# Graph layers before a routed FFN: two unread 512-column matmuls behind every group's products in layer one

## The chip, the cores and the metric

The kernel runs on one core of a Trainium2 chip. The metric is the device time of one launch in microseconds. The kernel before takes 6100.4 us, the median of three runs (6088.14, 6100.40 and 6104.39 us). The engines are called by their profile names: PE (TensorE), DVE (VectorE), ACT (ScalarE), POOL (GpSimd) and SP (SyncE).

## The reference

The input is x with 12500 nodes of 256 features, and 200000 edges sorted by destination, each with a source, a destination and a weight. What is computed, in float32:

```
def _gcn_layer(x, W, b, edge_weight, edge_src, edge_dst):
    support = x @ W
    msgs = support[edge_src] * edge_weight[:, None]
    agg = jax.ops.segment_sum(msgs, edge_dst, num_segments=N_NODES)
    return agg + b
h = elu(_gcn_layer(layernorm(x), W1, b1, ...)); h = elu(_gcn_layer(h, W2, b2, ...)); x = x + h
H = gelu(layernorm(x) @ ffn_W1 + b1)             # 1024 wide
probs = softmax(H @ Wg + bg); expert = argmax(probs)   # 8 experts
x = x + probs[expert] * (H @ Wd[expert] + bd[expert])
```

## The kernel before

The kernel applies the weights after the sum over edges, so a layer first sums the weighted source rows of each destination and then multiplies by W.

**Groups.** The edges are cut into 392 groups of 512 (`GE`), processed from the highest destination to the lowest. The `rows` tile has 8 slots (`SLOTS`), one for each group in flight. For every group POOL issues four indirect DMAs (L537), each of which gathers 128 rows of 256 floats from `xn_scratch` (layer one) or `h_scratch` (layer two) into the group's slot. Before the four it waits on L534 until the group that used the slot before, eight groups earlier, has been multiplied (semaphore `s_mm`).

**Products.** DVE builds four matrices S of 128 edges by 96 destinations (L853, `build_S`). PE multiplies them with the gathered rows, eight matmuls of 96 columns a group (L1170, `products`), into one of two banks of `pA`; the last one raises `s_mm`. DVE then adds the bank into the window of 192 numbers a partition in `aggT` (L892) and builds S for the group two further on. PE's products for a group wait for its rows, its S, and for the add of two groups earlier (L1226 to L1234). If a group's destinations go beyond its window, an extra product and add follow (`overflow`, the branch with `with_overflow`); the trace shows no time in that part that the argument needs.

**Halves and ticks.** Four groups make a half, of which a layer has 98 (`NH`). After a half every engine may run ticks, one for a block of 128 nodes whose sums are complete: layer one has one tick a half nearly everywhere. In a tick of layer one ACT copies the block into `stage` (L630) after the last add of the half, PE multiplies it with W1 into `pZ` (L1180, two matmuls of 256 columns), and ACT and DVE do bias and elu of the block before and store it through SP to `h_scratch`. PE's tick stands behind the half's fourth products and ahead of the next half's first ones. In layer two a tick also carries the FFN's first matmul, the gate and the stores. After both layers the nodes are sorted by expert and the second FFN matmul runs (L1282, L1292).

Each engine's program is written out in its own order, and semaphores join them. The two PSUM banks of `pB` hold the transposed edge tables before layer one (L1154) and the FFN's hidden block in layer two (L1208); layer one itself uses neither.

Of the kernel before, what the change touches and what calls it, by code (L numbers as in the profile page):

```python
# [7 lines left out]
def bass_gnn_then_routed_ffn(  # L8
# [92 lines left out]
    with ctx:  # L101
        def sb(name, shape, dt=f32):
            return ctx.enter_context(nc.sbuf_tensor(name, shape, dt))

        def ps(name, shape):
            return ctx.enter_context(nc.psum_tensor(name, shape, f32))
# [21 lines left out]
        w1 = sb("w1", [P, KC, HID])  # L128
# [5 lines left out]
        ident = sb("ident", [P, P])  # L134
# [80 lines left out]
        pB = ps("pB", [P, 1024])  # L215
# [141 lines left out]
        def half_flags(eng, h):  # L357

            v = eng.value_load(regs[0:1, bass.ds(h, 1), 0], min_val=0, max_val=(1 << 17) - 1)  # L359
            return v >> 16, (v >> 8) & 255, v & 255  # L360

        def overflow_windows(eng, g):
            ws = eng.value_load(wins[0:1, bass.ds(g, 1), 0], min_val=0, max_val=NG * P)
            we = eng.value_load(wins[0:1, bass.ds(g, 1), 1], min_val=0, max_val=NG * P)
            return ws, we
# [217 lines left out]
        def _(act):  # L583
# [89 lines left out]
            for layer in range(2):  # L673
                with act.Fori(0, ITERS) as i:
                    for half in range(2):
                        h = 2 * i + half
                        _, start, end = half_flags(act, h)
                        ticks(act, start, end, lambda j: (tick1, tick2)[layer](j, h))
                if layer == 0:
                    tick1(NB, None)  # L680
# [449 lines left out]
        def _(pe):  # L1130
            mm = nc.tensor.matmul
# [5 lines left out]
            for c in range(GCH):  # L1137
                cnt = P if c < GCH - 1 else TAILG
                at = NG - c * P - cnt
                for to, vector in zip(pROW, (gvec(0), gvec(1), gvec(3))):  # L1140
                    last = mm(to[:, at:at + cnt], vector[0:cnt, c:c + 1], flip[0:cnt, P - cnt:P],
                              start=True, stop=True)
# [4 lines left out]
            n = 0  # L1147
# [18 lines left out]
            def products(slot, Sx, to, semaphore):  # L1166

                for k in range(KC):
                    for t in range(T):
                        last = mm(to[:, k * W:(k + 1) * W], rows[:, slot, t, k * P:(k + 1) * P], Sx[:, t, :],  # L1170
                                  start=(t == 0), stop=(t == T - 1))
                last.then_inc(semaphore, 1)

            def z_part(layer, j):

                wg = (wg1, wg2)[layer]
                pe.wait_ge(s_stage[layer], j + 2)
                pe.wait_ge(s_zb[layer], j + 2)
                for k in range(KC):
                    last = mm(pZ[:, 0:C], stage[:, k, :], wg[:, k, :], start=(k == 0), stop=(k == KC - 1))  # L1180
                last.then_inc(s_z[layer], 1)

            def tick1(j):
                z_part(0, j)

            def tick2(j):
# [24 lines left out]
                if flows(0, j):  # L1211
                    z_part(1, j)
# [10 lines left out]
            def edges_half(layer, i, h, half, with_overflow):  # L1223
                for u in range(HALF):
                    s, g = half * HALF + u, HALF * h + u
                    pe.wait_ge(s_gath[layer][s], 16 * T * (i + 1))  # L1226
                    if with_overflow:
                        ws, we = overflow_windows(pe, g)
                        with pe.If(ws < we):
                            with pe.Fori(ws, we) as w:  # L1230
                                pe.wait_ge(s_ovS[layer], w + 1)
                                products(s, Sov, pOV, s_ovmm[layer])
                    pe.wait_ge(s_S[layer], g + 1)
                    pe.wait_ge(s_add[layer], g + 1)  # L1234
                    products(s, S[:, s % 2, :, :], pA[:, s % 2, :], s_mm[layer])

            pe.wait_ge(s_w, 8 * 16)
            for layer in range(2):
                with pe.Fori(0, ITERS) as i:
                    for half in range(2):  # L1240
                        h = 2 * i + half
                        ovf, start, end = half_flags(pe, h)
                        with pe.If(ovf > 0):
                            edges_half(layer, i, h, half, True)
                        with pe.Else():
                            edges_half(layer, i, h, half, False)
                        ticks(pe, start, end, (tick1, tick2)[layer])
# [16 lines left out]
            for i in runs(pe, NB // (2 * LB)):  # L1264
                for n in range(2):
                    pe.wait_ge(s_tile, 2 * i + n + 1)
                    pe.wait_ge(s_tgate, 2 * i + n + 1)
                    for k in range(LB):
                        outer = isinstance(i, int)
                        last = mm(pL, lane_is[:, n, k, :], tile_is[:, n, k, :, :].rearrange("p v n -> p (v n)"),  # L1270
                                  start=(outer and i == 0 and n == 0 and k == 0),
                                  stop=(outer and i > 0 and n == 1 and k == LB - 1))
# [53 lines left out]
```

## Time and profile before

| | us |
|---|---|
| median of three runs | 6100.4 |
| the profiled execution's own time | 6100.27 |
| its span, first to last instruction | 6098.5 |
| layer one, from POOL's first gather | about 95 to 2535 |
| layer two | about 2535 to 5500 |
| sorting and experts | about 5500 to 6098 |

Busy shares of the span are PE 59%, PE's weight loads 55%, POOL 53%, DVE 33% and ACT 18%. The profile's time starts at the first instruction. A busy time of PE counts from an instruction's start to a modelled end, and each float32 matmul of the program shows as two records, so a group's eight matmuls are 16 records. An "x64" on L1170 is the products of four groups. The number in brackets behind a row of the timeline is the engine's idle time just ahead of it, with what ended it; "remote" means that the releaser's record was not found.

### The profile page before, as it was taken

The numbers are of one execution on the slowest core, as the hardware profiler recorded it, in microseconds if no ns is written. First come the engines' busy times: TensorE is split into PE (matmuls) and PEld (weight loads), VectorE is DVE, ScalarE is ACT, GpSimd is POOL, SyncE is SP. The second block draws the span as 40 slices with busy tenths as digits, with TensorE's granted clock in tenths as the row PEclk, the third lists the DMA queues.
The fourth block names the chain that finished last, engine by engine and source line by source line (L and its number), as shares of the span: only waits on it lengthen the run. The fifth ranks groups of instructions, "written<-read, shape, count | busy, mean of one in ns | idle before, by whom it ended". The sixth has DMA issues, their size and how long they took to land.

```text
span 6098.5 us, 84880 instructions
## 1 busy us (share of the span) xinstructions
PE 3582.9 (59%) x21458; PEld 3351.2 (55%) x21459; DVE 2006.6 (33%) x6596; ACT 1122.0 (18%) x1692; POOL 3256.1 (53%) x3403
## 2 busy tenths in 40 slices
PE   2455555455555545466556556555656555566999
PEld 2454445444544445465555555555556555565888
DVE  6222222222222222233333333333333333336333
ACT  3111111111111111032222222222222222221111
POOL 5566666566666666545555445545555554542444
PEclk6666666666666666677777777777777777778999
DMA  7333333333333333223333333333333333323554
GB/s 235 87 94 91 91 92 92 88 93 91 92 93 89 92 89 93 77 81 97 99 96 98 96 100 95 97 94 98 97 97 96 97 97 95 97 84 108 179 177 157
DMA packets 266659, 627.26 MB, mean 103 GB/s; under 512 B 63397, under 2 KB 135034, under 8 KB 265922
## 3 DMA queue, kind: packets, MB, share of 16 engines
q0 software_dynamic: 170688, 492.87, 27.9%
q1 hardware_dynamic: 95362, 129.30, 6.0%
q14 instruction: 597, 4.89, 0.3%
q8 instruction: 12, 0.20, 0.0%
HBM read 519.25 MB, written 103.63 MB: 102 GB/s over the span
## 4 chain that ended last, share of the span: by engine, by line
issue 30%; PE 25%; another core or an unknown queue 21%; DVE 10%; DVEq 9%; ACT 3%; ACTq 1%; DMA 1%; POOL 0%; SPq 0%; POOLq 0%
PE pA L1170 12%; PE pA L1292 6%; DVE S L853 4%; PE pB L1208 3%; DVEq L359 1%; DVEq L882 1%; PE pZ L1180 1%; DVE aggT L892 1%; DVEq L853 1%; DVEq L892 1%; DVEq L975 1%; PE pC L1282 1%; PE pB L1282 1%; DVEq L370 1%
## 5 line engine op out<-in xcount | busy, mean ns | idle before, releaser
L537 POOL DMA_INDIRECT rows<-h_scratch,idx x1568 | 1488.8, 949 | 1474.3 <-PE pA L1170 830.9
L1170 PE MATMUL pA<-S,rows 128*128 128x96 f32 x12544 | 1891.1, 323 | 509.0 <-DVE S L853 331.2
L1170 PEld LDWEIGHTS pA<-S,rows 128*128 128x128 f32 x12544 | 1850.2, 238 | 593.7 <-DVE S L853 442.7
L537 POOL DMA_INDIRECT rows<-xn_scratch,idx x1568 | 1491.9, 951 | 924.2 <-issue 429.0
L892 DVE TENSOR_TENSOR aggT<-aggT,pA 128x192 f32 x784 | 277.4, 354 | 3280.6 <-remote 1591.5
L630 ACT ACT_TABLE_LOAD x196 | 251.5, 1283 | 4195.9 <-DVE aggT L892 2838.8
L853 DVE TENSOR_SCALAR S<-iota_p,tdst,twgt 128x96 f32<-128x96 f32 x3152 | 861.1, 343 | 12.3 <-issue 9.1
L1180 PE MATMUL pZ<-wg,stage 128*128 128x256 f32 x784 | 311.1, 537 | 855.5 <-ACT stage L630 609.4
L1180 PEld LDWEIGHTS pZ<-wg,stage 128*128 128x128 f32 x784 | 186.5, 263 | 896.1 <-ACT stage L630 621.2
L1208 PE MATMUL pB<-work,w 128*128 128x128 f32 x3232 | 592.6, 361 | 72.5 <-issue 71.2
L1198 PE MATMUL pT<-ident,work 128*128 128x128 f32 x206 | 67.9, 431 | 943.8 <-DVE work L930 703.4
L1208 PEld LDWEIGHTS pB<-work,w 128*128 128x128 f32 x3232 | 568.5, 274 | 82.8 <-issue 81.5
L1198 PEld LDWEIGHTS pT<-ident,work 128*128 128x128 f32 x206 | 29.1, 196 | 963.9 <-DVE work L930 717.8
L1292 PE MATMUL pA<-aggT,work 128*128 x1680 | 382.9, 381 | 0.2
L1292 PEld LDWEIGHTS pA<-aggT,work 128*128 128x128 f32 x1680 | 312.1, 191 | 40.5 <-issue 1.1
L567 POOL DMA_INDIRECT out_dram<-aggT,ids x105 | 107.3, 1022 | 227.3 <-DVE ids L1093 180.5
L1192 PE MATMUL pC<-identg,work 128*128 128x136 f32 x1236 | 166.3, 283 | 22.7 <-issue 20.2
L1192 PEld LDWEIGHTS pC<-identg,work 128*128 128x128 f32 x1236 | 152.7, 191 | 24.0 <-issue 21.2
L1111 DVE TENSOR_TENSOR aggT<-pA,aggT 128x256 f32<-128x256 f32 x105 | 44.6, 425 | 277.2 <-PE pA L1292 222.9
L669 ACT ACT_TABLE_LOAD x100 | 128.3, 1283 | 8.2 <-remote 6.4
L658 ACT ACT_TABLE_LOAD x100 | 128.3, 1283 | 1.8
L935 DVE TENSOR_TENSOR work<-pB,b1col 128x1024 f32<-128x1024 f32 x102 | 123.9, 1214 | 3.3 <-PE pB L1208 2.4
(173 smaller groups left out, 2286.3 us busy)
## 6 DMA issues: line engine op xcount, KB each, us to landing
pay_scratch<-work SPq DMA_DIRECT2D x98, 512.0 KB
rows<-xn_scratch,idx POOLq DMA_INDIRECT x1568
rows<-h_scratch,idx POOLq DMA_INDIRECT x1568
h_scratch<-work SPq DMA_DIRECT2D x98, 128.0 KB
pay_scratch<-work SPq DMA_DIRECT2D x98, 128.0 KB
work<-in_x_dram SPq DMA_DIRECT2D x97, 128.0 KB
rows<-in_x_dram SPq DMA_DIRECT2D x24, 512.0 KB, 5.3
xn_scratch<-rows SPq DMA_DIRECT2D x24, 512.0 KB, 5.7
```

The source lines that it names most:

```text
L537: pool.indirect_dma_start(rows[:, s, t, :], None, source, bass.IndirectOffsetOnAxis(at, 0))\
L630: act.activation(stage[:, :, :], aggT[:, :, block_of(j)], ACT.Copy).then_inc(s_stage[layer], 1)
L658: act.activation(bstd[:, 0:1], bmv[:, 1:2], ACT.Sqrt, bias=epsc[:, :]).then_inc(s_std2, 1)
L669: act.activation(HT, hid, ACT.Gelu).then_inc(s_gelu, 1)
L853: last = v.tensor_scalar(S[:, half, t, :], iota_w[:, :], tdst[:, t, bass.ds(g, 1)], twgt[:, t, bass.ds(g, 1)], ALU.is_equal, ALU.mult)
L892: v.tensor_tensor(to, to, pA[:, u % 2, 0:KC * W].rearrange("p (k n) -> p k n", k=KC), ALU.add)\
L935: v.tensor_tensor(hid, pB[:, :].rearrange("p (k n) -> p k n", k=KH), b1col[:, :].unsqueeze(2).to_broadcast([P, KH, P]), ALU.add).then_inc( ...
L1170: last = mm(to[:, k * W:(k + 1) * W], rows[:, slot, t, k * P:(k + 1) * P], Sx[:, t, :], start=(t == 0), stop=(t == T - 1))
L1180: last = mm(pZ[:, 0:C], stage[:, k, :], wg[:, k, :], start=(k == 0), stop=(k == KC - 1))
L1192: mm(pF[:, m // PERB, m % PERB, :], HT[:, m, :], identg[:, m, :], start=True, stop=True)
L1208: last = mm(pB[:, m * P:(m + 1) * P], w1[:, k, m * P:(m + 1) * P], xnT[:, k, :], start=(k == 0), stop=(k == KC - 1))
L1292: last = mm(pA[:, q % 2, 0:C], HTx[:, q % 2, m, :], wdk[:, m, bass.ds(ec, C)], start=(m == 0), stop=(m == KH - 1))
```

## The change

A function `keep_running` is added, and in layer one PE calls it behind the products of each group. It multiplies the 128x128 identity matrix with the first 1024 columns of `w1`, in two matmuls of 512 columns, into the two banks of `pB`. Nobody waits for them and nobody reads what they write; they raise no semaphore and wait for none. The group's `s_mm` is still raised by the last matmul of the products ahead of them. The call stands in `edges_half`, in both branches.

```
+            def keep_running():
+
+                for n in range(2):
+                    mm(pB[:, n * 512:(n + 1) * 512], ident[:, :], w1[:, 0, n * 512:(n + 1) * 512], start=True, stop=True)
+
@@
                     pe.wait_ge(s_S[layer], g + 1)
                     pe.wait_ge(s_add[layer], g + 1)
                     products(s, S[:, s % 2, :, :], pA[:, s % 2, :], s_mm[layer])
+                    if layer == 0:
+                        keep_running()
```

The first place is on PE, inside a half of layer one without overflow: the end of the skipped branch, then the first two groups. Before:

```order
L1243 UNCONDITIONAL_BRANCH
L1226 ISA
L1233 REGISTER_ALU
L1170 MATMUL pA<-S,rows 128x96 x8
L1233 REGISTER_ALU
```

And after, with the lines below the new function moved down:

```order
L1250 UNCONDITIONAL_BRANCH
L1231 ISA
L1238 REGISTER_ALU
L1170 MATMUL pA<-S,rows 128x96 x8
L1177 MATMUL pB<-w,ident 128x512 x2
L1238 REGISTER_ALU
```

The second group's wait for its rows (the `REGISTER_ALU` with the gather's semaphore) and its products now stand behind two matmuls of 512 columns.

The second place is on PE at the end of a half, where `pZ<-wg,stage` is the tick's matmul. Before:

```order
L1233 REGISTER_ALU
L1170 MATMUL pA<-S,rows 128x96 x8
L1245 UNCONDITIONAL_BRANCH
L369 REGISTER_ALU x3
L369 COMPARE_AND_BRANCH
L370 UNCONDITIONAL_BRANCH
L370 ISA
L1180 MATMUL pZ<-wg,stage 128x256 x2
```

And after:

```order
L1238 REGISTER_ALU
L1170 MATMUL pA<-S,rows 128x96 x8
L1177 MATMUL pB<-w,ident 128x512 x2
L1252 UNCONDITIONAL_BRANCH
L369 REGISTER_ALU x3
L369 COMPARE_AND_BRANCH
L370 UNCONDITIONAL_BRANCH
L370 ISA
L1185 MATMUL pZ<-wg,stage 128x256 x2
```

The fourth group's extra matmuls stand between its products and the tick, whose matmul waits for `stage` in both kernels. The order on DVE, ACT, POOL and SP is unchanged.

## Rows read from the trace of the kernel before

**Rows 1.** The page's head: busy time of PE, and granted clock by slice.

```profile
span 6098.5 us, 84880 instructions
...
PEclk6666666666666666677777777777777777778999
```

**Rows 2.** Busy by stage; last three columns: granted clock, DMA share, GB/s.

```profile
95.00:2535.00 2440.00, 1259.40 (x6664) 1159.74 (x6664) 675.59 (x2411) 269.42 (x493) 1488.63 (x1566) 0.67 0.32 91
2535.00:5500.00 2965.00, 1764.19 (x11731) 1696.46 (x11732) 993.84 (x3324) 718.20 (x976) 1488.49 (x1568) 0.76 0.31 95
```

**Rows 3.** Groups of layer one: busy, mean ns, idle before, releasers.

```profile
L537 POOL DMA_INDIRECT rows<-xn_scratch,idx x1565 | 1488.8, 951 | 915.8 <-issue 420.6 <-PE pA L1170 290.8 <-remote 194.3
L1170 PE MATMUL pA<-S,rows 128*128 128x96 f32 x6272 | 1066.3, 350 | 336.1 <-DVE S L853 230.3 <-DVE aggT L892 77.2 <-issue 27.1
L1180 PE MATMUL pZ<-wg,stage 128*128 128x256 f32 x392 | 203.0, 673 | 855.5 <-ACT stage L630 609.4 <-issue 170.7 <-DVE zb L901 75.3
L892 DVE TENSOR_TENSOR aggT<-aggT,pA 128x192 f32 x392 | 138.3, 353 | 1617.5 <-remote 782.7 <-PE pA L1170 460.8 <-issue 374.0
```

**Rows 4.** Timeline of one half of layer one: start, length, what, idle before.

```profile
1536.91 0.35 DVE L892 TENSOR_TENSOR aggT<-aggT,pA 128x192 f32 x1 [5.80 <-remote]
...
1537.50 0.95 POOL L537 DMA_INDIRECT rows<-xn_scratch,idx  x1 [2.44 <-remote]
...
1539.29 2.08 PE L1180 MATMUL pZ<-wg,stage 128*128 128x256 f32 x4 [10.25 <-ACT stage L630]
...
1541.16 9.26 PE L1170 MATMUL pA<-S,rows 128*128 128x96 f32 x64
1541.26 0.95 POOL L537 DMA_INDIRECT rows<-xn_scratch,idx  x1 [0.30 <-issue]
1544.95 0.35 DVE L892 TENSOR_TENSOR aggT<-aggT,pA 128x192 f32 x1 [4.09 <-PE pA L1170]
...
1545.52 0.95 POOL L537 DMA_INDIRECT rows<-xn_scratch,idx  x1 [3.30 <-PE pA L1170]
...
1547.02 0.35 DVE L892 TENSOR_TENSOR aggT<-aggT,pA 128x192 f32 x1 [0.53 <-PE pA L1170]
...
1550.52 0.95 POOL L537 DMA_INDIRECT rows<-xn_scratch,idx  x1 [0.30 <-issue]
1551.40 0.35 DVE L892 TENSOR_TENSOR aggT<-aggT,pA 128x192 f32 x1 [3.07 <-PE pA L1170]
...
1559.30 0.95 POOL L537 DMA_INDIRECT rows<-xn_scratch,idx  x1 [0.30 <-issue]
1562.71 0.35 DVE L892 TENSOR_TENSOR aggT<-aggT,pA 128x192 f32 x1 [9.95 <-remote]
```

**Rows 5.** Stretches of that half; columns as in Rows 2.

```profile
1541.20:1544.70 3.50, 3.50 (x18) 3.50 (x18) 0.00 (x0) 0.00 (x0) 0.95 (x1) 0.50 0.39 115
1544.70:1550.40 5.70, 5.70 (x49) 5.55 (x47) 2.86 (x10) 0.00 (x0) 3.79 (x4) 0.95 0.25 70
1545.00:1547.00 2.00, 2.00 (x19) 2.00 (x18) 1.49 (x5) 0.00 (x0) 1.18 (x2) 0.94 0.00 0
1547.00:1561.90 14.90, 3.41 (x31) 3.25 (x29) 2.67 (x10) 0.00 (x0) 10.20 (x11) 0.67 0.37 106
1562.00:1564.00 2.00, 0.00 (x0) 0.00 (x0) 1.29 (x6) 0.67 (x1) 0.70 (x1) 0.50 0.00 0
```

**Rows 6.** L1180 in layer one: duration ns, least, median, most.

```profile
L1180 PE MATMUL pZ<-wg,stage x392: 597/634/796, 150.8 to 2526.5; 128*128 128x256 f32 x196
```

**Rows 7.** L1292 in the experts' stage, 256 columns; columns as in Rows 3.

```profile
L1292 PE MATMUL pA<-aggT,work 128*128 x1680 | 382.9, 381 | 0.2
```

**Rows 8.** Timeline of layer two; columns as in Rows 4.

```profile
4025.08 3.81 PE L1170 MATMUL pA<-S,rows 128*128 128x96 f32 x32 [1.29 <-DVE S L853]
...
4031.61 0.35 DVE L892 TENSOR_TENSOR aggT<-aggT,pA 128x192 f32 x1 [5.33 <-remote]
...
4032.20 0.95 POOL L537 DMA_INDIRECT rows<-h_scratch,idx  x1 [0.94 <-remote]
```

## The prediction

> **What bounds the kernel now.** I read the busy time by stage first. Layer one takes 2440 us from POOL's first gather, with PE busy for 1259 us, a mean granted clock of 0.67 and the DMA engines at 32% [rows 2]. Neither PE nor the DMA engines fill it; clock and span are those of [rows 1].
>
> Then the groups of that stage. POOL's 1565 gathers there have 1488.8 us busy and 915.8 us idle [rows 3]. A gather is 0.951 us, and the usual gap behind it is 0.30 us [rows 4], so the 16 gathers of a half cost 20.0 us if nothing stops them. A half really takes (1488.8 + 915.8) / 1565 x 16 = 24.6 us. So POOL's issue is the base of the time, and about 4.6 us a half, 450 us in 98 halves, are stops of POOL. It stops only for a free slot, and slots are freed by PE's `s_mm`.
>
> Then one half in order of time [rows 4]. Call its groups g0 to g3. The last add of the half before starts at 1536.91, and POOL resumes at 1537.50. ACT stages the block, PE starts the tick's matmul at 1539.29 and the products of g0 at 1541.16; DVE adds g0 at 1544.95 and POOL resumes at 1545.52, after a stop of 3.30 us. PE goes straight through all four groups, 64 records in 9.26 us, so it is done at 1550.4. POOL meanwhile issues twelve gathers without a stop, to 1560.25. The add of g3 comes at 1562.71, 12.3 us after PE's last record, and with it the next half starts. So a half is: add of g3, to g0's products seen (8.0 us between POOL's two restarts), three groups of gathers, and the wait until g3 is seen.
>
> The reader is to see that finished products are noticed at once in some places and late in others. With 16 records each, at 3.50 us for 18 of them and then 5.70 us for 49 [rows 5], g0 ends at about 1544.6, g1 at 1546.7, g2 at 1548.6 and g3 at 1550.4. A waiting add starts some 0.2 us after it is released. So g0 and g1 are seen at once (adds 1544.95, 1547.02), g2 about 2.6 us late (1551.40) and g3 12 us late. The DMA engines moved nothing from 1545.0 to 1547.0, 106 GB/s from 1547.0 to 1561.9, and nothing after 1562 [rows 5]: g1 is noticed in a pause of the gathers, g2 and g3 ended while gathers were landing. Layer two has the same: 32 records start at 4025.08 and last 3.81 us, so the first group of the two ends near 4027.1, its add comes only at 4031.61, and POOL, which had stopped for it, resumes at 4032.20 [rows 8]. That is 4.3 us late. "Remote" as releaser of 782.7 us of DVE's waits for adds [rows 3] fits this.
>
> The Trainium skill says in "Perfetto Trace Analysis", section "Tensor Engine Instruction (MATMUL, LD_WEIGHTS)", that TensorE's ends are estimated and that the semaphore update leaves when PSUM has acknowledged the writes. The trace agrees that the two differ, by up to 12 us in the half above; the page gives no cause and no figure for it.
>
> **The change part by part.** Nothing is removed. Each group gets two float32 matmuls of 512 columns, four records. At the high clock the nearest row is the experts' 256-column matmul, 382.9 us / 1680 = 0.228 us a record [rows 7]; twice the columns is 0.456, so 1.8 us a group. At the low clock it is the tick's matmul, also 256 columns, 203.0 / 392 = 0.518 us [rows 3], so 4.1 us a group. In the half above the clock is 0.50 during g0 and 0.95 from 1544.7 on [rows 5]. So I take 2.1 us behind g0 (0.5 us of it low) and 1.8 us behind g1 to g3, 7.5 us a half. PE is busy 1259 / 98 = 12.9 us of 24.6 now [rows 2], so the work itself fits: 20.4 of 24.6.
>
> *Behind g3.* The extra 1.8 us lie in the time in which PE waits for the stage, 10.25 us ahead of the tick [rows 4]. Cost nothing; if g3 were seen at once, 2.4 us (add to tick's matmul) would still cover them.
>
> *Behind g2.* They delay g3. g3 ends near 1550.4 now and is needed by POOL at 1560.3. Covered by 10 us.
>
> *Behind g0.* They delay the products of g1, whose wait for rows and whose matmuls are queued behind them on PE. g0's own `s_mm` is raised before them. g1 ends at 1548.8 instead of 1546.7. POOL needs g1 for its gather at 1550.52, so by about 1550.2. If it is seen at once, the cost is 0, the lower bound. But the pause of the gathers is over at 1547.0, and g1 now ends where g2 did. With g2's lateness of 2.6 us it is seen at 1551.4 to 1551.5, and POOL resumes 0.8 us later (4031.4 to 4032.20 in layer two): 1552.3 instead of 1550.52, +1.8 us. With layer two's 4.3 us it is +3.5 us, the upper bound. I take g2's lateness as the nearest row, and in 60% of the halves, since the slack of 1.4 us covers the smaller delays: 1.1 us a half.
>
> *Behind g1.* g2 starts up to 1.8 us later than its place behind g1. POOL needs it a group of gathers later than g1, 5.0 us, and is itself later by then. Nothing in the forecast; in the rival with every group late it costs.
>
> *The clock.* Extra work on PE could hold the high clock over the wait, so that the tick's matmul and g0 run faster: 2.08 / 2 = 1.0 us, and for g0 3.3 - 1.9 = 1.4 us, together 2.4 us a half off the stop of 3.30. The rows speak against it: over 1547.0 to 1561.9 the clock is 0.67 [rows 5], which is 5 us high and 10 low, so it fell near 1552, within 2 us of PE's end. The 392 records of L1180 in layer one have a least duration of 597 ns [rows 6], against 381 ns mean for as many columns at the high clock [rows 7]. PE's idle time before the tick shrinks from 12 us ahead of this add by 7.5 us at most, and stays longer than what the clock survived here. I take 0.
>
> In "TensorE: Matmul & The Clock Gate", section "Why this matters for your kernels", the Trainium skill says to keep TensorE continuously busy for the high clock and without long gaps between bursts. That speaks for the change: with the gap filled, the sum would be 98 x 2.4 us less, the first rival. The trace agrees with it on the fall after idleness, and no row here shows whether the shorter gap is short enough.
>
> **The sum.** Made against the profiled execution, 6100.3 us (span 6098.5 and 1.8 around it), which is the median of the runs within 0.1 us. 98 x 1.1 = 108 us, all in layer one; layer two has no added work. 6100 + 108 = 6208 us. With the bounds of g1's cost, 0 and 3.5 us, it is 6100 to 6443.
>
> **Rivals.**
> - *The clock stays high through the tick (faster).* For it: less idle time ahead of the tick. Against it: [rows 5, 6] as above. It decides from the point where the clock is high at the tick's matmul; 2.4 x 98 = 235 us less, 5865 us.
> - *g3 is seen early (faster).* If what follows on PE brings a finished group to notice, the extra matmuls behind g3 do that, and the tick hides beside POOL's gathers: 24.6 falls to 20.0 + 0.6, 98 x 4.0 = 392 less, 5708 us. Against it: g2 has work right behind it now and is late, in both layers.
> - *All hidden.* g1 is seen within its slack of 1.4 us: 6100 us.
> - *Every group is late.* With g1 seen in the flow, g2 and g3 each bring a stop of their own as in layer two, 0.94 - 0.30 = 0.6 us each: 1.8 + 0.6 + 0.6 = 3.0 us a half, 294 us, 6394 us.
> - *PE becomes the bound.* If the clock stayed low, a half on PE is 4 x (3.3 + 4.1) + 2.1 + 2.4 = 34.1 us, 9.5 more: 931 us, 7030 us. Against it: the clock rises now with less work on PE.
>
> **How the numbers follow.** Forecast 0.43 (own range 6130 to 6290), high clock 0.09, g3 early 0.04, all hidden 0.17, every group late 0.23, PE the bound 0.04. A measurement of this kernel tells about 0.3%, 18 us, from no change. So faster 0.13, same 0.18 (all hidden and the forecast's edge), slower 0.69. The range runs from 6085, which takes in the hidden case, to 6400, which takes in the case of every group late; left out are the two faster rivals, the bound PE and edges, less than 2 in 10.
>
> **What would show it.** Right: L1177 with 1568 records in layer one, near 0.45 to 0.6 us apart; the add of g1 later by 3 us or more after g0's, and a stop of POOL before its gathers behind g1 that isn't there now; L1180 still with durations near 634 ns; layer two unchanged. Wrong: POOL's idle time in layer one at 916 us or below, L1180 with a median near 400 ns (the clock), or the add of g3 soon after its products.

## The result and the profile after

The changed kernel takes 6119.6 us (median of 12 runs, 6113.0 to 6139.4), the kernel before on the same chip 6103.1 us (12 runs, 6087.7 to 6115.1). The ratio is 1.0034, 95% interval 1.0022 to 1.0045: 17 us slower, where 108 were forecast. Both profiled executions lie off those medians, the one before 3 us under it (6100.3) and the one after 12 us over it (6131.8), so the traces differ by 32 us and the medians by 17.

The page's head after the change, which answers to [rows 1]:

```profile
span 6130.1 us, 88016 instructions
...
PE 4080.0 (67%) x23026; PEld 3438.5 (56%) x23027; DVE 2010.8 (33%) x6596; ACT 1121.3 (18%) x1692; POOL 3247.1 (53%) x3403
...
PEclk7878888888788888777777777777777777778999
```

The two layers, columns as in [rows 2] (after the length: busy us of PE, weight loads, DVE, ACT and POOL, then granted clock, DMA share, GB/s):

```profile
95.00:2560.00 2465.00, 1765.88 (x8212) 1254.58 (x8213) 673.41 (x2386) 264.60 (x485) 1482.55 (x1564) 0.82 0.31 89
2560.00:5535.00 2975.00, 1761.29 (x11764) 1693.53 (x11764) 999.80 (x3351) 723.47 (x986) 1485.42 (x1568) 0.77 0.31 95
```

And the groups of layer one, which answer to [rows 3], with the duration of the tick's matmul, which answers to [rows 6]:

```profile
L537 POOL DMA_INDIRECT rows<-xn_scratch,idx x1564 | 1482.6, 948 | 958.2 <-issue 424.7 <-PE pA L1170 305.9 <-remote 218.5
L1170 PE MATMUL pA<-S,rows 128*128 128x96 f32 x6260 | 904.5, 306 | 108.7 <-issue 50.0 <-DVE S L853 47.2 <-DVE aggT L892 10.6
L1177 PE MATMUL pB<-w,ident 128*128 128x512 f32 x1564 | 805.7, 640 | 0.7 <-issue 0.7
L1185 PE MATMUL pZ<-wg,stage 128*128 128x256 f32 x388 | 175.4, 598 | 609.5 <-ACT stage L630 515.2 <-issue 69.1 <-DVE zb L901 25.2
```

```profile
L1185 PE MATMUL pZ<-wg,stage x388: 379/634/796, 152.1 to 2530.5; 128*128 128x256 f32 x194
```

Three things are to be seen. PE has 507 us more of busy time in layer one and its mean clock there rises from 0.67 to 0.82. The tick's matmul now has a least duration of 379 ns where it had 597, but its median stays at 634 ns: only some ticks find a high clock. And POOL's idle time in layer one goes from 915.8 to 958.2 us, 42 us more, while its busy time there is 6 us less; together that is 36 us, and the traces differ by 32. So the loss is again where [rows 3] had the whole slack: in POOL's stops for a free slot.

**Where the stops lie.** From the start times of L537's 1568 records I took every half, from its first group's first gather to the next half's, and every gap that exceeds the usual 0.30 us by more than 0.3. A half can have such a stop ahead of each of its four slots, and it waits there for g0, g1, g2 or g3 of the half whose slots it takes over. Mean stop by slot, in us, over 96 halves:

| | first (g0) | second (g1) | third (g2) | fourth (g3) | sum |
|---|---|---|---|---|---|
| before | 3.10 | 0.06 | 0.30 | 0.98 | 4.4 |
| after | 2.80 | 0.10 | 0.77 | 1.15 | 4.8 |

The forecast's stop, at the second slot, is not there: 2 halves had one before, 4 have one now. What grew is the stop at the third slot. It is in 46 halves instead of 21. The stop at the fourth slot grew as well in this pair of traces, by 0.17 us, and the one for g0 shrank by 0.30.

Here is a half of the kernel after with it (start, length, what, idle time before it and its releaser, as in [rows 4]; some rows left out):

```profile
1137.30 0.94 POOL L537 DMA_INDIRECT rows<-xn_scratch,idx  x1 [2.90 <-PE pA L1170]
1138.10 1.92 PE L1170 MATMUL pA<-S,rows 128*128 128x96 f32 x16
...
1139.85 1.91 PE L1177 MATMUL pB<-w,ident 128*128 128x512 f32 x4
1140.35 0.35 DVE L892 TENSOR_TENSOR aggT<-aggT,pA 128x192 f32 x1 [7.29 <-PE pA L1170]
...
1141.58 0.34 DVE L892 TENSOR_TENSOR aggT<-aggT,pA 128x192 f32 x1
1141.71 2.02 PE L1170 MATMUL pA<-S,rows 128*128 128x96 f32 x16
...
1145.32 1.92 PE L1170 MATMUL pA<-S,rows 128*128 128x96 f32 x16
1146.06 0.95 POOL L537 DMA_INDIRECT rows<-xn_scratch,idx  x1 [0.30 <-issue]
...
1148.86 0.35 DVE L892 TENSOR_TENSOR aggT<-aggT,pA 128x192 f32 x1 [5.84 <-remote]
...
1149.43 0.95 POOL L537 DMA_INDIRECT rows<-xn_scratch,idx  x1 [2.42 <-remote]
1150.09 0.34 DVE L892 TENSOR_TENSOR aggT<-aggT,pA 128x192 f32 x1
...
1161.55 0.94 POOL L537 DMA_INDIRECT rows<-xn_scratch,idx  x1 [2.41 <-PE pA L1170]
```

g1 and its add are in time (1141.58). g0's add comes 3 us after POOL went on by the same semaphore; there it is DVE that is late, whose sequencer stands 3.6 and 1.8 us behind the branches between two halves (L975, L979), so g0's notice is dated by POOL and not by its add. g2's products start at 1141.71, when the unread matmuls behind g1 and g2's own S (complete at 1141.67) are both done, so only a part of its delay is the change's. g2 ends on PE at 1143.7, 6.4 us after POOL resumed, and is added only at 1148.86. POOL had come to the third slot at 1147.0 and stood still for 2.42 us. In that stop g3 is noticed too (its add is at 1150.09, 2.8 us after its products), so the fourth slot costs nothing, and the next stop is 2.41 us. The half takes 24.25 us.

What the DMA engines moved around that stop, columns as in [rows 5]:

```profile
1143.70:1147.30 3.60, 3.60 (x22) 2.64 (x21) 0.00 (x0) 0.00 (x0) 2.69 (x3) 1.00 0.38 109
1147.30:1148.20 0.90, 0.90 (x3) 0.38 (x3) 0.00 (x0) 0.00 (x0) 0.00 (x0) 1.00 0.45 127
1148.20:1149.40 1.20, 0.79 (x2) 0.00 (x0) 0.54 (x3) 0.00 (x0) 0.00 (x0) 1.00 0.04 14
```

The last gathers land for a microsecond more, then the transfers cease, and within it the two late groups are noticed. "Noticed" is not to be taken as one engine looking too late: the waits of POOL and of DVE for g2's semaphore end at the same moment, 1148.68, as they do for g3 in [rows 4], 1562.55. The signal itself comes late.

And a half of the same kernel with the other kind of stop:

```profile
1536.24 0.95 POOL L537 DMA_INDIRECT rows<-xn_scratch,idx  x1 [3.23 <-PE pA L1170]
...
1542.18 1.92 PE L1170 MATMUL pA<-S,rows 128*128 128x96 f32 x16
...
1550.04 0.95 POOL L537 DMA_INDIRECT rows<-xn_scratch,idx  x1 [0.30 <-issue]
1553.33 0.35 DVE L892 TENSOR_TENSOR aggT<-aggT,pA 128x192 f32 x1 [11.06 <-remote]
...
1553.92 0.94 POOL L537 DMA_INDIRECT rows<-xn_scratch,idx  x1 [2.93 <-remote]
...
1561.37 0.35 DVE L892 TENSOR_TENSOR aggT<-aggT,pA 128x192 f32 x1 [4.10 <-PE pA L1170]
...
1561.94 0.94 POOL L537 DMA_INDIRECT rows<-xn_scratch,idx  x1 [3.33 <-PE pA L1170]
```

Here g3's products start at 1542.18 and end near 1544, no stop comes in the flow, and g3 is noticed 9 us late, when POOL stops for it ahead of the fourth slot (2.93 us). Only then can the tick begin, and the stop for g0 is 3.33 us. The half takes 25.70 us.

**Kinds of half.** Sorted by that, over 95 halves (count x mean us of one):

| | second slot | third only | third and fourth | fourth only | neither | mean |
|---|---|---|---|---|---|---|
| before | 2 x 25.2 | 11 x 24.2 | 10 x 25.5 | 32 x 25.5 | 40 x 23.9 | 24.66 |
| after | 4 x 25.3 | 32 x 24.3 | 13 x 26.0 | 30 x 25.9 | 16 x 24.1 | 25.04 |

A half with a stop at the third slot alone is only 0.2 to 0.3 us longer than one without, since the stop for g0 behind it is shorter, and 1.3 to 1.6 us shorter than one that stops at the fourth slot. The half in [rows 4], on which the forecast was built, starts with POOL's restart at 1545.52 and stops at the fourth slot alone:

```profile
1563.30 0.95 POOL L537 DMA_INDIRECT rows<-xn_scratch,idx  x1 [3.05 <-remote]
...
1570.90 0.95 POOL L537 DMA_INDIRECT rows<-xn_scratch,idx  x1 [2.90 <-PE pA L1170]
```

It takes 25.38 us and is of a dear kind, which a third of the halves belong to in both kernels. What has become rare is the cheapest kind, without a stop in the flow, of which the forecast had no example.

### The profile page after: what moved, and what is told of

It reads as the page before. It is cut to its first block, busy times and chain, and to the rows that moved or that the text cites. A ratio compares the mean times of both kernels' runs of the same rounds, so it can differ in the third digit from the quotient of the medians.

```text
span 6130.1 us, 88016 instructions
## 1 busy us (share of the span) xinstructions
PE 4080.0 (67%) x23026; PEld 3438.5 (56%) x23027; DVE 2010.8 (33%) x6596; ACT 1121.3 (18%) x1692; POOL 3247.1 (53%) x3403
## 4 chain that ended last, share of the span: by engine, by line
PE 38%; another core or an unknown queue 22%; issue 21%; DVE 10%; DVEq 5%; ACT 3%; DMA 1%; ACTq 1%; POOL 0%; SPq 0%; POOLq 0%
PE pA L1170 17%; PE pB L1177 7%; PE pA L1299 6%; DVE S L853 4%; PE pB L1213 3%; PE pZ L1185 3%; DVE aggT L892 1%; DVEq L882 1%; DVEq L853 1%; DVEq L892 1%; PE pC L1289 1%; ACT stage L630 1%; PE pB L1289 1%; DVEq L359 1%
## 5 line engine op out<-in xcount | busy, mean ns | idle before, releaser
L537 POOL DMA_INDIRECT rows<-h_scratch,idx x1568 | 1485.4, 947 | 1474.7 <-PE pA L1170 809.4
L1170 PEld LDWEIGHTS pA<-S,rows 128*128 128x128 f32 x12544 | 1710.5, 218 | 533.8 <-issue 309.0
L537 POOL DMA_INDIRECT rows<-xn_scratch,idx x1568 | 1486.6, 948 | 967.3 <-issue 433.7
L1170 PE MATMUL pA<-S,rows 128*128 128x96 f32 x12544 | 1740.7, 302 | 306.8 <-DVE S L853 180.7
L1177 PE MATMUL pB<-w,ident 128*128 128x512 f32 x1568 | 807.6, 640 | 0.7 <-issue 0.7
L1185 PE MATMUL pZ<-wg,stage 128*128 128x256 f32 x784 | 282.7, 496 | 610.3 <-ACT stage L630 516.0
L1213 PE MATMUL pB<-work,w 128*128 128x128 f32 x3232 | 579.4, 356 | 64.8 <-issue 62.1
L1185 PEld LDWEIGHTS pZ<-wg,stage 128*128 128x128 f32 x784 | 170.9, 242 | 711.1 <-ACT stage L630 582.1
L1177 PEld LDWEIGHTS pB<-w,ident 128*128 128x128 f32 x1568 | 295.6, 210 | 211.6 <-issue 211.6
```

Of the source, the lines that this page charges most:

```text
L537: pool.indirect_dma_start(rows[:, s, t, :], None, source, bass.IndirectOffsetOnAxis(at, 0))\
L1177: mm(pB[:, n * 512:(n + 1) * 512], ident[:, :], w1[:, 0, n * 512:(n + 1) * 512], start=True, stop=True)
L1213: last = mm(pB[:, m * P:(m + 1) * P], w1[:, k, m * P:(m + 1) * P], xnT[:, k, :], start=(k == 0), stop=(k == KC - 1))
```

## The experiments

Kernels that are compared ran in one session on one chip, together with the kernel before, and ratios are to it. There were two sorts of session, and what could be told apart depended on them: in two the kernel before takes 4711 and 4726 us, in the others 6103 to 6203 us. In the fast sort finished products are noticed at once, and POOL has next to no stops in layer one to gain or lose.

**One part of the change at a time, in a session of the fast sort (kernel before 4726.3 us).** The call gets a condition on the group, `u == 3`, `u < 3`, `u == 0`, `u == 1`:

```
-                    if layer == 0:
+                    if layer == 0 and u == 3:
                         keep_running()
```

Behind the fourth group alone:

> The two extra matmuls stand behind the fourth group of a half (g3) alone, 98 places in place of 392. Theory A (the change is a sum of two small terms: g2's products later, which adds 0.48 us of POOL stops a half, and a faster tick in some halves, which takes 0.26 us): the first term is gone, so -5 to -25 us against before, if the 1.8 us behind g3 alone are enough to lift the clock at the tick; else 0. Theory B (the forecast's: g1 is noticed late at 1.8 us a half, and a gain of the clock of nearly the same size hides it): the gain stands alone, -80 us or more. Theory C (none of the places matters, the 17 us are a property of the whole): within 10 us of the full change.

Behind the first three:

> The extra matmuls stand behind g0, g1 and g2 and not behind g3. Theory A: g2's delay is all there, and the idle time of PE ahead of the tick is 1.8 us longer than with the full change: +20 to +55 us against before, more than the full change, with the tick's matmul at the low clock nearly everywhere. Theory B: +100 us. Theory C: as the full change, +17 us.

Behind the first alone:

> The extra matmuls stand behind g0 alone. g1 is delayed by about 2 us, g2 hardly, since it waits for its S. Theory A: -10 to +15 us against before. Theory B (g1 seen late, +1.8 us in most halves): +60 to +110 us, with POOL's stops ahead of the gathers into g1's slot.

Behind the second alone:

> The extra matmuls stand behind g1 alone, so g1's end stays and g2 may start up to 1.8 us later, but only as far as it does not wait for its S anyway. Theory A: 0 to +25 us against before, all of it in stops ahead of the gathers into g2's slot. Theory B: 0.

Measured, in that order: 4724.8 us, ratio 0.9995 (0.9984 to 1.0006); 4731.9, 1.0009 (0.9995 to 1.0024); 4726.0, 1.0002 (0.9990 to 1.0015); 4731.8, 1.0007 (0.9996 to 1.0017). POOL's gathers in layer one with the first of them:

```profile
L537 POOL DMA_INDIRECT rows<-xn_scratch,idx x1565 | 1486.2, 950 | 476.7 <-issue 471.5 <-PE pA L1170 5.2
```

Of 476.7 us idle 471.5 are the usual gaps. A half is 20.06 us, the 20.0 us of POOL's issuing that the forecast worked out. What follows: where products are noticed at once the extra matmuls cost nothing that can be told from noise (all four intervals take in 1). Of the forecast only its lower bound, no cost if g1 is seen at once, could be judged here, and it holds.

**Size of the edit, and the tick (kernel before 6198.6 us).** In a session of the slow sort: the kernel before once more, the whole change, four unread matmuls behind each group in place of two, and ten behind the fourth group alone.

```
-                for n in range(2):
-                    mm(pB[:, n * 512:(n + 1) * 512], ...)
+                for n in range(4):
+                    b = n % 2
+                    mm(pB[:, b * 512:(b + 1) * 512], ...)
```

> The kernel before, for its trace under the conditions of the four runs so far, in which it took 4726 us and not 6103. Theory P (where finished products are noticed at once, POOL's issue sets the pace of layer one): the adds start 0.2 us after the products' end, POOL has next to no stops, and a half is 16 x 1.255 = 20.1 us, layer one about 1968 us. Rival: products are noticed as late as in the first trace, and the gathers are what is faster. If this run takes about 6100 us instead, late notice is back and its trace is one more of that kind.

> The full change, in one call with the kernel before. Theory P: where before takes 4726 us, PE's extra 7.5 us a half lie in PE's waits for gathers, so 0 to +10 us; where before takes 6100 us, +17 us again. Rival Q (each extra matmul costs its own small price, whatever the pace of the rest): +17 us, 0.3%, in both.

> Four extra matmuls behind every group in place of two. A half then needs of PE 4 x (1.8 + 3.6) + 1.0 for the tick + 2.4 from the last add to the tick's matmul = 25 us, above the 20.1 us of POOL's issue. Theory P: where before takes 4726 us, PE becomes the bound: +4 to +6 us a half, 390 to 590 us. Where before takes 6100 us: a half is 24.6 us already and loses 1 to 5 us, 100 to 500 us. Rival (the extra matmuls run beside the products): under 30 us in either.

> Ten extra matmuls behind g3 alone, 9 us at the high clock, to fill PE's wait ahead of the tick. Where before takes 6100 us: the tick's matmul and g0 run at the high clock nearly everywhere and the forecast's first rival is tested: -2.4 us a half, -235 us, if faster products are noticed sooner; 0 if their notice hangs on POOL's gathers. Where before takes 4726 us: g3 is noticed at once, so 9 us of unread work stand ahead of the tick; a half on PE is 4 x 1.8 + 9 + 1 = 17 us plus its waits, +0 to +2.5 us a half, up to 250 us.

Measured: the kernel before 6197.9; the whole change 6208.5, ratio 1.0024 (1.0010 to 1.0039), so the result repeats; with four 6258.8, 1.0100 (1.0070 to 1.0129); with ten behind the fourth 6249.3, 1.0075 (1.0047 to 1.0102). Stops by slot and kinds of half:

| | first | second | third | fourth | second slot | third only | third and fourth | fourth only | neither |
|---|---|---|---|---|---|---|---|---|---|
| before | 3.08 | 0.04 | 0.44 | 1.31 | 1 | 24 | 2 | 45 | 23 |
| whole change | 2.76 | 0.07 | 0.99 | 1.10 | 3 | 44 | 0 | 39 | 9 |
| four | 2.65 | 0.50 | 0.96 | 1.32 | 35 | 32 | 3 | 24 | 1 |
| ten, fourth only | 3.06 | 0.01 | 0.24 | 2.07 | 0 | 9 | 10 | 63 | 13 |

The gathers' rows of layer one for these four, in this order:

```profile
L537 POOL DMA_INDIRECT rows<-xn_scratch,idx x1566 | 1483.9, 948 | 961.1 <-issue 414.8 <-PE pA L1170 300.8 <-remote 233.0
```

```profile
L537 POOL DMA_INDIRECT rows<-xn_scratch,idx x1565 | 1484.7, 949 | 963.7 <-issue 424.2 <-remote 269.0 <-PE pA L1170 261.6
```

```profile
L537 POOL DMA_INDIRECT rows<-xn_scratch,idx x1565 | 1482.4, 947 | 1018.9 <-issue 414.3 <-remote 303.1 <-PE pA L1170 289.7
```

```profile
L537 POOL DMA_INDIRECT rows<-xn_scratch,idx x1566 | 1485.8, 949 | 1008.0 <-issue 405.6 <-PE pA L1170 341.6 <-remote 242.5
```

What follows. The stops at the second slot, which the forecast expected from two matmuls, come with four, when the second group ends 3.3 us later behind the first than in the kernel before, and then only in 35 of 95 halves. Unread work behind the fourth group doesn't bring it to notice: its add comes 9.2 us after its products on average, 7.5 without. The tick's matmul found a high clock in 28% of the halves with two, in 69% with four, in 47% with ten behind the fourth, and in none before. With four the mean stop for g0 is 0.43 us shorter than before, and the kernel is slower all the same. With ten behind the fourth, where the first rival's gain of 235 us was at stake, that stop is 3.06 us against 3.08, so nothing came of it; and with four the price is 60 us, below the 100 to 500 that were expected.

**One part at a time in a session of the slow sort (kernel before 6192.9 us).** The kernels with `u == 0` and `u == 1` again, one with `u == 2`, and one with four matmuls at `u == 0`:

> The extra pair stands behind the first group's products alone, so the second group ends 1.9 us later in the half with nothing unread behind it. Theory A (a group is noticed on time in the early flow because unread work stands right behind it on PE): here the second group has its successor's waiting products behind it, as in the kernel before, and is noticed 1 to 2 us late in most halves; POOL's stops at the second group's slot rise from 0.05 to 0.8 to 1.2 us a half, +80 to +110 us. Theory B (only the place of a group's end in POOL's flow of gathers counts; within 4 us of POOL's restart a late notice is still covered): stops at the second group's slot stay under 0.2 us, those at the third group's rise a little because it is pushed too, by 0.3 us a half; 0 to +30 us. Where this chip notices products at once (kernel before near 4726 us), both expect 0 within 10 us.

> The extra pair stands behind the second group's products alone; the third and fourth groups end 1.9 us later. Theory A: the second group is noticed sooner, the third unchanged in manner; time within 15 us of the kernel before. Theory B: the third group's end moves from 4.8 to 5.5 to 6.5 us behind POOL's restart, where the traces so far show a stop more often, so stops at the third group's slot rise by 0.4 to 0.6 us a half, +40 to +60 us. Where this chip notices products at once, both expect 0 within 10 us.

> The extra pair stands behind the third group's products alone; only the fourth ends 1.9 us later. Theory A: stops at the third group's slot go down, by up to 0.3 us a half, and the time is 0 to 30 us less. Theory B: the third group ends where it did, its stops stay at 0.3 to 0.45 us a half; the fourth ends later in the flow and its stops rise by 0 to 0.2 us a half; 0 to +20 us. Where this chip notices products at once, both expect 0 within 10 us.

> Four extra matmuls instead of two behind the first group alone, none behind the others: the second group ends about 3.8 us later, near 6 us behind POOL's restart. Theory A: the second group is noticed late in most halves, stops at its slot 1.5 us or more a half, +150 us. Theory B: it now ends where the third group does in the whole change (5.5 to 6 us), so a stop in about half of the halves: 0.5 to 1.0 us a half at its slot and 0.3 to 0.5 more at the third's, +80 to +140 us. With four behind every group the stops at the second slot were 0.50 us a half. Where this chip notices products at once, both expect 0 to +30 us.

Measured:

| unread matmuls | us | ratio | first | second | third | fourth | third only | fourth only | neither |
|---|---|---|---|---|---|---|---|---|---|
| behind g0 | 6167.0 | 0.9952 (0.9935 to 0.9969) | 3.03 | 0.10 | 0.76 | 0.80 | 32 | 28 | 26 |
| behind g1 | 6189.4 | 0.9991 (0.9977 to 1.0004) | 3.06 | 0.03 | 0.57 | 1.13 | 27 | 41 | 26 |
| behind g2 | 6247.2 | 1.0088 (1.0066 to 1.0111) | 2.94 | 0.01 | 0.34 | 2.07 | 15 | 66 | 6 |
| four behind g0 | 6196.3 | 1.0003 (0.9989 to 1.0017) | 3.01 | 0.49 | 0.47 | 1.18 | 13 | 33 | 7 |

(In the last, 37 halves stop at the second slot.) The gathers' rows of the first and the third:

```profile
L537 POOL DMA_INDIRECT rows<-xn_scratch,idx x1565 | 1484.2, 948 | 942.8 <-issue 422.1 <-PE pA L1170 281.9 <-remote 230.6
```

```profile
L537 POOL DMA_INDIRECT rows<-xn_scratch,idx x1564 | 1485.9, 950 | 1006.6 <-issue 398.3 <-PE pA L1170 309.1 <-remote 281.9
```

Theory A, by which work standing right behind a group brings it to notice, falls: with nothing unread behind the second group its stops stay at 0.10 us where 0.8 to 1.2 were expected. Theory B had the places of the stops right for `u == 0` (0.76 at the third slot against 0.44, none new at the second); for `u == 1` the rise was 0.13 where it expected 0.4 to 0.6, and for `u == 2` the stops at the fourth slot rose by 0.76 where it expected 0.2 at most. What they cost it had wrong: it expected 0 to 30 us more behind g0 and 40 to 60 more behind g1, and the kernel is 26 us faster in the one case and unchanged in the other. Behind g2 it expected 0 to 20 us and there are 54. For four behind g0 both theories expected 80 us or more, and the kernel is unchanged, though 37 of 95 halves now stop at the second slot. So the part that the forecast charged with the whole loss makes the kernel faster when it stands alone, and a part that it put down as covered by 10 us is the dear one. In both cases the time goes with the stops at the fourth slot, not with those at the third: 66 halves that stop at the fourth slot alone with `u == 2`, 28 with `u == 0`. No trace of the kernel before was taken beside these four, so the comparison of kinds is with the one above, whose median is 6 us off.

**A stop by force.** If a stop at the third slot takes the place of a later one, one forced into every half should cost nearly nothing. POOL fills a part of a tile that layer one doesn't use, and waits for the end of it:

```
                     for s in range(SLOTS):
                         g = SLOTS * i + s
...
+                        if layer == 0 and s % HALF == 2:
+                            pool.wait_ge(s_S[0], 1)
+                            pool.memset(work[:, 0:2048], 0.0).then_inc(s_pause, 1)
+                            hold(pool, s_pause, 2 * i + s // HALF + 1)
                         hold(pool, s_mm[layer], g + 1)
```

With it went the same ahead of the fourth slot (`s % HALF == 3`), the whole change with the forced stop, and the kernel before with gathers of 64 columns in place of 256 in layer one (`rows[:, s, t, 0:64]` from rows a quarter as long), which leaves the other 192 columns out of layer one's gathers:

> The kernel before, with a fill of 2048 numbers a partition on POOL and a wait for its end ahead of the third group's gathers in every half of layer one (about 1.9 us, from 307 ns for 256 numbers): a forced stop. Theory S (stops take each other's place: whoever stops ahead of the third slot doesn't stop ahead of the fourth, and stops 0.8 us less behind the first group): nearly all halves become of the kind seen with a stop there, 24.3 to 24.5 us, against a mix of 24.7 to 25.0 now: 20 to 60 us less than before. Theory N (stops add up): +1.9 x 98 = +186 us. Where this chip notices products at once (kernel before near 4726 us), POOL never stops in layer one, and both expect about +190 us.

> The same forced stop ahead of the fourth group's gathers instead. Theory S: nearly all halves become of the kind with a stop there, 25.5 to 25.9 us, against 24.7 to 25.0 now: +60 to +110 us, though the forced stop is as long as the other. Theory N: +186 us. Where products are noticed at once, both expect about +190 us.

> The whole change together with the forced stop ahead of the third slot. Theory S: with a stop in every half at that place the change has nothing left to bring about; within 10 us of the same kernel without the unread matmuls (p3_pause), or up to 20 us less where the tick's matmul finds a high clock. Theory N: +186 and +17 us over the kernel before.

> The kernel before, but layer one's gathers move 64 numbers of a row in place of 256, a quarter of the bytes with as many descriptors and as many instructions of POOL; the other columns of the slots keep what they held. If the late notice goes with the bytes in flight: products are noticed at once or within 1 us, POOL's stops in layer one fall from 4.3 to 4.8 us a half to under 1.5 us, 300 us less or more. If it goes with POOL's issuing or with the number of descriptors: stops stay near 4.5 us a half, within 50 us of the kernel before. Where this chip notices products at once, 0 within 30 us.

These fell in a session of the fast sort (kernel before 4711.2 us) and told nothing apart but the price of a stop where there are no others: 4972.3 us, ratio 1.0557 (1.0542 to 1.0572), which is 2.66 us a half; 4963.1, 1.0538 (1.0521 to 1.0554); 4976.6, 1.0564 (1.0548 to 1.0580); 4702.6, 0.9979 (0.9969 to 0.9989). Whether the late notice goes with the bytes of the gathers was not to be seen there, and stays open.

So the forced stop was run again, a little shorter (`work[:, 0:1792]`), first ahead of the third slot, then of the fourth, and both sessions were of the slow sort:

> The forced stop ahead of the third slot again, with a fill of 1792 numbers a partition (by the 1822 ns of 2048 numbers 1.6 us, with the wait behind it about 2.4 us a half where POOL never stops otherwise). Where products are noticed late: theory S (stops take each other's place) has halves of 24.4 to 24.8 us with no further stop ahead of the fourth slot, between 60 us less and 10 us more than the kernel before; theory N (stops add up) has +2.4 x 98 = +235 us. Where products are noticed at once, both expect +235 us and nothing is told apart.

> The forced stop (fill of 1792 numbers, 2.3 us with the wait) ahead of the fourth slot instead of the third. Where products are noticed late: if the place sets the price, nearly all halves are like those that now stop there, 25.4 to 25.9 us against 24.7 to 25.1, +50 to +100 us; if any forced stop takes away the others, as the one ahead of the third slot did, within 30 us of the kernel before; if stops add up, +225 us. Where products are noticed at once, about +230 us and nothing is told apart.

Ahead of the third slot: 6179.0 us against 6196.7, ratio 0.9969 (0.9958 to 0.9979), 18 us faster, with a fill of 1.6 us in each of 98 halves. Stops that would add up were to cost 235 us. Ahead of the fourth: 6251.8 against 6203.3, ratio 1.0068 (1.0042 to 1.0094), 48 us slower. By slot, the forced stop among them:

| forced stop | first | second | third | fourth | sum | mean half |
|---|---|---|---|---|---|---|
| ahead of the third | 1.27 | 0.97 | 2.30 | 0.01 | 4.6 | 24.86 |
| ahead of the fourth | 1.64 | 0.01 | 1.11 | 2.52 | 5.3 | 25.52 |
| none, another session | 3.08 | 0.04 | 0.44 | 1.31 | 4.9 | 25.04 |

POOL's groups of layer one, the forced stop ahead of the third slot:

```profile
L542 POOL DMA_INDIRECT rows<-xn_scratch,idx x1563 | 1482.7, 949 | 782.0 <-issue 441.5 <-remote 248.2 <-PE pA L1175 50.8
L537 POOL MEMSET work<- 128x1792 f32 x98 | 157.7, 1609 | 14.7 <-DVE S L858 14.7
```

And one half of it:

```profile
1415.23 0.94 POOL L542 DMA_INDIRECT rows<-xn_scratch,idx  x1 [2.59 <-PE pA L1175]
...
1416.26 5.44 PE L1175 MATMUL pA<-S,rows 128*128 128x96 f32 x32 [3.05 <-DVE aggT L897]
...
1424.94 1.61 POOL L537 MEMSET work<- 128x1792 f32 x1
1426.87 0.35 DVE L897 TENSOR_TENSOR aggT<-aggT,pA 128x192 f32 x1 [6.90 <-remote]
...
1427.49 0.95 POOL L542 DMA_INDIRECT rows<-xn_scratch,idx  x1 [0.94 <-remote]
...
1429.25 2.08 PE L1185 MATMUL pZ<-wg,stage 128*128 128x256 f32 x4 [7.55 <-ACT stage L635]
...
1432.50 0.95 POOL L542 DMA_INDIRECT rows<-xn_scratch,idx  x1 [0.30 <-issue]
...
1439.78 0.94 POOL L542 DMA_INDIRECT rows<-xn_scratch,idx  x1 [2.58 <-remote]
```

The fourth group's products end at 1421.7, and its add waits until the fill has held up the gathers: 1426.87. The tick follows 2.4 us later, POOL passes the fourth slot without a stop (1432.50, 0.30 us), and the next stop is 2.58 us. This half takes 24.55 us. The fill puts 2.30 us into a half, and the other stops sum to 2.25 us instead of 4.87. Of 95 halves one stops at the fourth slot; 35 stop at the second, which hardly one did before.

So it is shown that POOL's stops replace one another, and that what one costs depends on its place: ahead of the third slot it is free, or better, ahead of the fourth it is dear, where moreover the stops at the third slot rise from 0.44 to 1.11 us. The stretches above suggest why: what is late is noticed when the gathers cease, so a half needs such a pause somewhere, and it is best had as soon as the late groups' products are done. That reading rests on the order of events in the traces and was not tried by itself, and one event speaks against it as a rule: in [rows 4] g2 was noticed (its add is at 1551.40) while POOL issued without a stop, and in the 0.4 us up to 1551.20 the DMA engines moved 184 GB/s.

## Why the prediction was right and wrong

**The time.** 6208 us forecast, 6119.6 measured. The direction was right and the time is inside the range; the size was six times too large, 108 us against 17. The direction came out right by luck: the one term that carried it makes the kernel faster when it stands alone, and a term that the forecast put at nothing makes it slower.

**Extra matmuls by themselves.** Right. L1177 has four records a group, 1568 in all. From group to group PE takes 3.50 us at the high clock where it took 1.79, so 1.7 us a group against the forecast's 1.8.

**"Behind g0."** The step that failed. It put g1's lateness at 1.8 us in 60% of the halves, and so 1.1 us a half. Three things were wrong in it. The late group was not g1: in nine halves of ten it ended less than 3.3 us after POOL's restart, and its slot's mean stop went from 0.06 to 0.10 us. The group that became late was g2. In both traces no half had a stop at the third slot when g2 ended less than 5 us after the restart, and 17 of 23 before and 40 of 46 after had one when it ended over 6 us after it; the median end moved from 4.8 to 5.7 us. This is no rule for all kernels here: with the matmuls behind g0 alone 13 of 60 halves stopped there though g2 had ended before 5 us. That stop is 0.5 us a half more. And the price was taken as if all other stops stayed: in the session that traced both kernels together it was 0.55 more at the third slot and 0.21 less at the fourth, 0.32 less at the first (in the first pair of traces 0.47 more, 0.17 more and 0.30 less). With the term alone, unread matmuls behind g0 and nowhere else, the kernel is 26 us faster; by the forecast it should have been 108 us slower. The forced stop shows the exchange without the matmuls.

**"Behind g1: nothing."** Right within its interval (0.9991, 0.9977 to 1.0004).

**"Behind g2: covered by 10 us."** Wrong alone, 54 us. The 10 us were right for PE's end, but not for its notice: g3 was already late by 12 us in [rows 4], and pushed further it misses the fourth slot more often, 66 halves of 95. In the whole change this seems to be partly taken away by the stops at the third slot: 39 halves stop at the fourth alone, against 45, in the pair of traces from one session. The three parts run alone in the slow sort, 26 us less, 3 less and 54 more, sum to 25 us more, and the whole change measures 17 and 10 us; so the loss is in the main the part behind g2, less what the part behind g0 gives back. How the parts act on one another was not measured.

**"Behind g3: nothing."** Not run with two matmuls in a session of the slow sort. Ten cost 51 us there; why its stops then rise at the fourth slot is open, since g3's products end no later.

**"The clock: 0."** Too small, though the reason was half right. In 29% of the halves the tick's matmul now runs at the high clock, and the mean stop for g0 is 0.3 us less. The most of that goes with the exchange of stops: in the kernel before, where no tick runs at the high clock, the stop for g0 is 1.76 us behind a half that stopped at the third slot alone and 3.45 us behind one that did not stop. Within the halves of that kind in the kernel after it is 2.27 us with the tick at the low clock (12 halves) and 1.81 with it at the high one (20), so the clock gives some 0.5 us in a fifth of the halves, 0.1 us a half, an estimate from these two means. The Trainium skill, in "TensorE: Matmul & The Clock Gate", section "Why this matters for your kernels", advises to keep TensorE busy without long gaps. The trace agrees that filling the gap raises the clock (0.67 to 0.82 in layer one). The section speaks of matmul throughput, and here the kernel's time did not follow: it was 17 us more.

**The rivals.** Clock high through the tick, g3 seen early, every group late and PE the bound did not come. "All hidden" was nearest in time (6100) and wrong in its reason, since stops did move. None of my cases had the stops exchanging.

## What to carry to other kernels

Where one engine stops several times in a period for others, don't add a new stop to the old ones: ask which of the old ones it makes needless. Count the kinds of period over the whole stage before taking one of them as the pattern; the half that the forecast was built on was one kind of five, and the change worked by moving halves from one kind to another. A wait for work that is long done, as g3 was in [rows 4], is not shortened by doing the work sooner; what a stop costs at a given place can be measured by one put in by force.

## What the runs showed of the hardware

- The same kernel takes 4711 or 4726 us in two sessions and 6103 to 6203 us in five others. The chip had the number 2 in one session of either sort (4711 and 6203 us), so this is either no property of the chip or the number doesn't name it. The difference is POOL's stops: in layer one 5 us of idle time beyond the usual gaps in the one sort, near 500 us in the other. Layer two has the larger share: POOL's idle time ahead of its gathers is 539 us there with the unread matmuls behind g3 alone in the fast sort, and 1474 us in the kernel before in the slow one; nothing is added to layer two in either.
- In the slow sort a group of layer one that ends 5.5 us or more after POOL has resumed its gathers is noticed over 2 us late in 83 to 100% of the cases in the twelve traces of that sort, with a median of 3 to 8 us. Of the groups that end over 2 us after POOL has stopped, 0 to 6% are noticed over 1 us late, by the time of their semaphore's signal, in the ten of these traces without a forced stop. What holds the notice up is not settled.
- The same kind of forced stop made the kernel 18 us faster in a session of the slow sort (2.30 us in a half) and 261 us slower in one of the fast sort (2.66 us).
- The best version measured has the two unread matmuls behind the first group of each half alone: 0.9952 (0.9935 to 0.9969) in the slow sort and 1.0002 (0.9990 to 1.0015) in the fast one.
